# Gated cross-attention with a dense expert layer: the output projection as three fp32r products, and new places for the units beside the attention

## The chip, the core and the metric

The kernel runs on one core of a Trainium2 chip. The metric is the device time of one execution in microseconds (us). The engines of the core run their own instruction streams and meet at semaphores: TensorE (PE; its weight loads are listed apart, as PEld), VectorE (DVE), ScalarE (ACT), GpSimd (POOL) and SyncE (SP), which here issues all DMAs.

## The reference, cut to what matters

Batch 8, 512 queries and 512 keys for each, 256 channels, 16 heads of 16 channels, 8 experts with 1024 hidden channels. All is fp32.

```
def xattn(query, kv):
    q, k, v = query @ Wq + bq, kv @ Wk + bk, kv @ Wv + bv     # 16 heads of 16
    attn = softmax(clip(q @ k.T / 4, -1e4, 1e4))
    return (attn @ v) @ Wo + bo                               # output projection
x = x + tanh(g_xattn) * xattn(layernorm(x), ctx)
n = layernorm(x)
logits = n @ gate_weight.T                                    # kept if not under the 6144th smallest of 32768
y_e = gelu(n @ w1_e.T + b1_e) @ w2_e.T + b2_e                 # all 8 experts, dense
x = x + tanh(g_ffn) * sum_e(y_e * gate_e)
```

## The kernel before, in words

There are three stages. The first (lines 68 to 482) makes q, k and v of all batches and stores them in memory; each product is taken there in **fp32r**, a form of fp32 that TensorE takes in one pass with fewer bits, as three products of high and low parts (high by high, high by low, low by high), since operands are split by ScalarE (a copy into fp32r, the high part) and VectorE (the difference, the low part). The third stage is the experts, from about 560 us on.

The change is in the second stage, the attention (`attend_programs`, from line 643). For each of 8 batches it runs 4 groups `g` of 4 heads, each in 4 steps `k`, each with 4 places: 64 places in a batch, named `(g, k, place)`. At each place

- PE writes one turned score tile of the batch at hand into `ps_t` (line 862) and one score tile of 8 steps ahead into `ps_s` (line 851);
- ACT takes the exponential of the `ps_t` tile (line 1170, into `probs_T` or `w_raw`);
- DVE takes the least value of each row of the `ps_s` tile (`low`, line 1007).

`ps_t` and `ps_s` have 3 banks each, so PE can run three places ahead of ACT and DVE, no more. At place 3 of a step PE multiplies the probabilities of the step before by the values (`ps_o`, line 873, fp32).

All other work of a batch goes through one shared bank, `ps_m`, in units that are written into the stream at fixed places: the tables `SHARED` and `HALVES` say after which place PE writes a unit, `SCALAR_AT` and `VECTOR_AT` after which place ACT and DVE take it. Each entry is (kind, batch offset, index). The kinds: `low` (the least values, turned, line 879), `out` (heads turned, line 884, then normalised by DVE, lines 1025 to 1030), `rows` (the attention output turned, line 890, copied by ACT, line 1186), `y` (**the output projection**, line 898), after it DVE's residual add (line 1040), `statistics` (line 1048), `norm` (line 1082), the turned units `x2T` (905) and `xnT` (911), whose low part DVE makes (line 1091), `check` (lines 1013 and 1015), `logits` (919) and `pick` (926, once in four batches). Before a unit is written, PE waits for the unit before it in `ps_m` to be taken. The order on every engine is therefore written out by hand: an engine that waits at one unit holds up all that stands behind it.

The output projection before is one fp32 product: per batch 4 tiles of 128 queries by 2 halves of the channels, `attn_T` (fp32) by `wo` (fp32), 256 columns wide. TensorE carries each out as two recorded instructions. Two units `y` hold two tiles each; the first unit is cut into halves (`HALVES`), at two places. What belongs to the last batch has no further batch to lie beside: it is handed to the experts' programs as a list of closing pieces, and its units alternate between `ps_m` and `ps_o`.

`Wo` is loaded by SP in the first stage (line 175).

Of the kernel before, what the change touches and what calls it, by code (L numbers as in the profile page):

```python
# [549 lines left out]
VECTOR_AT = {  # L550
    (0, 1, 3): [("out", -1, 3)], (0, 2, 1): [("check", 0, 1)], (1, 0, 0): [("y", -1, 0)],
    (1, 0, 3): [("statistics", -1, 0), ("statistics", -1, 1)], (1, 1, 1): [("check", 0, 2), ("y", -1, 1)],
    (1, 1, 3): [("statistics", -1, 2), ("statistics", -1, 3)], (1, 2, 1): [("out", 0, 0)], (1, 3, 3): [("norm", -1, 0)],
    (2, 0, 1): [("norm", -1, 1)], (2, 0, 2): [("check", 0, 3)], (2, 1, 0): [("norm", -1, 2)], (2, 2, 1): [("out", 0, 1)],
    (2, 2, 2): [("norm", -1, 3)], (2, 3, 1): [("xnT", -1, 0)], (3, 1, 1): [("xnT", -1, 1)], (3, 2, 2): [("out", 0, 2)],
    (3, 3, 0): [("check", 1, 0)], (3, 3, 3): [("pick", -1, 0)],
# [3 lines left out]
    (0, 0, 3): [("copy", -1, 3), ("low", 0, 1)], (0, 2, 2): [("rows", -1, 0)], (0, 2, 3): [("rows", -1, 1)],  # L560
    (1, 1, 0): [("copy", 0, 0)], (1, 1, 2): [("low", 0, 2)], (1, 3, 2): [("x2T", -1, 0)],
    (2, 0, 3): [("x2T", -1, 1), ("copy", 0, 1)], (2, 1, 0): [("low", 0, 3)], (2, 3, 1): [("xnT", -1, 0)],
    (3, 0, 0): [("xnT", -1, 1)], (3, 0, 3): [("copy", 0, 2)], (3, 1, 2): [("low", 1, 0)], (3, 3, 0): [("logits", -1, 0)],
# [2341 lines left out]
```

## Time and profile before

| | us |
|---|---|
| median of 3 runs (lowest, highest) | 1897.73 (1895.09, 1897.74) |
| the profiled execution | 1896.23 |
| its span, first to last instruction | 1894.4 |
| PE busy, of the span | 1862.6 |
| DVE, ACT busy | 1291.1, 1277.7 |
| first stage | 0 to about 92 |
| attention | about 92 to 521 |
| experts | from there, alone from about 560 |

The page shows PE busy almost always. Matmuls are pipelined and their ends are modelled, so a full row of nines for PE does not say that PE has nothing to win or to lose: the spacing of its instructions and the idle time of the other engines have to be read beside it. TensorE's granted clock is at full speed except around 85 to 125 us.

### The profile page before, as it was taken

Reading aid. Unit: us, or ns where it says so; the run is one execution under the profiler, and the core shown is the slowest. Engines: PE = TensorE matmul, PEld = TensorE weight load, DVE = VectorE, ACT = ScalarE, POOL = GpSimd, SP = SyncE. Lnnn points to the kernel's source line nnn. Section 1 sums busy time; section 2 is a strip of 40 time slices with the busy share of each in tenths; the row PEclk is TensorE's granted clock in tenths of the full one; section 3 lists DMA queues with packets and bytes.
Section 4 is the critical chain, followed back from the end, with each engine's and each line's share of the span. In section 5 each row is a group of like instructions: output and inputs, shape, how many; then the busy total and the mean of one; then the engine's idle time right before and its main releaser. Section 6 shows DMA issues by size and latency. Waiting matters only on the chain.

```text
span 1894.4 us, 25738 instructions
## 1 busy us (share of the span) xinstructions
PE 1862.6 (98%) x8868; PEld 1349.0 (71%) x8868; DVE 1291.1 (68%) x2279; ACT 1277.7 (67%) x2145; POOL 146.9 (8%) x327
## 2 busy tenths in 40 slices
PE   7999999999999999999999999999999999999998
PEld 6844444444478777887888788788878888887886
DVE  6789999999666665656556666755665676556555
ACT  4447778777855556767666676766667676666665
POOL 6201101111135200000000000000000000000000
PEclk9969999999999999999999999999999999999999
DMA  8933333233113254333232333233233423222321
GB/s 284 374 81 84 87 91 88 79 88 110 38 50 129 107 210 151 119 117 110 90 111 89 133 138 124 95 112 112 89 112 129 151 93 117 111 90 89 121 101 58
DMA packets 97245, 220.84 MB, mean 117 GB/s; under 512 B 31314, under 2 KB 49492, under 8 KB 87892
## 3 DMA queue, kind: packets, MB, share of 16 engines
q1 hardware_dynamic: 97108, 219.12, 33.5%
q8 instruction: 73, 1.20, 0.3%
q14 instruction: 64, 0.52, 0.1%
HBM read 178.57 MB, written 40.24 MB: 116 GB/s over the span
## 4 chain that ended last, share of the span: by engine, by line
PE 89%; ACT 3%; DVE 2%; issue 1%; POOL 0%; ACTq 0%; DVEq 0%; POOLq 0%
PE ps_y L2169 32%; PE ps_h L2116 28%; PE ps_t L862 7%; PE ps_o L873 6%; PE ps_h L2089 5%; PE ps_y L2101 4%; PE ps_s L851 2%; PE ps_m L898 2%; PE ps_m L884 1%; ACT w_raw L1170 1%; DVE low L1007 1%; PE ps_m L890 0%; ACT gelu L2366 0%; PE ps_m L919 0%; PE ps_m L905 0%
## 5 line engine op out<-in xcount | busy, mean ns | idle before, releaser
L2469 DVE TENSOR_TENSOR h_lo<-gelu,h_hi 128x512 fp32r<-128x512 f32 x512 | 352.8, 693 | 437.0 <-ACT h_hi L2369 405.7
L2116 PE MATMUL ps_h<-x_hi,w_pair 128*128 128x512 f32 x1568 | 562.3, 392 | 1.8 <-ACT gelu L2366 0.8
L2366 ACT ACTIVATE gelu<-early,b 128x512 f32<-128x512 f32 x336 | 243.2, 724 | 229.5 <-DVE early L2618 220.7
L2116 PEld LDWEIGHTS ps_h<-x_hi,w_pair 128*128 128x128 f32 x1568 | 294.3, 188 | 78.3 <-issue 6.0
L1007 DVE TENSOR_REDUCE low<-ps_s 128x1 f32<-128x512 f32 x512 | 322.1, 681 | 26.1 <-PE ps_s L851 23.1
L2369 ACT ACTIVATE h_hi<-gelu 128x512 fp32r<-128x512 f32 x448 | 283.5, 633 | 41.9 <-ACT gelu L2366 1.1
L2116 PE MATMUL ps_h<-x_lo,w_pair 128*128 128x512 f32 x784 | 309.4, 395 | 0.0
L2618 DVE TENSOR_TENSOR early<-ps_h,copy 128x512 f32<-128x512 f32 x336 | 230.5, 686 | 49.4 <-PE ps_h L2116 49.4
L1170 ACT ACTIVATE probs_T<-ps_t 128x512 f32<-128x512 f32 x384 | 206.4, 594 | 45.5 <-PE ps_t L862 44.6
L851 PE MATMUL ps_s<-k_st,q_st 48*128 48x512 f32 x512 | 205.0, 481 | 3.2 <-SPq L755 2.0
L2169 PE MATMUL ps_y<-h_hi,w_lo 128*128 128x512 f32 x512 | 202.7, 396 | 0.0
L2169 PE MATMUL ps_y<-h_hi,w_hi 128*128 128x512 f32 x512 | 202.4, 395 | 0.0
L2169 PE MATMUL ps_y<-h_lo,w_hi 128*128 128x512 f32 x512 | 202.0, 394 | 0.0
L862 PE MATMUL ps_t<-q_st,k_st 49*128 49x512 f32 x512 | 190.4, 456 | 3.6 <-ACT probs_T L1170 2.7
L862 PEld LDWEIGHTS ps_t<-q_st,k_st 49*128 49x128 f32 x512 | 84.0, 188 | 131.8 <-ACT probs_T L1170 54.3
L2116 PEld LDWEIGHTS ps_h<-x_lo,w_pair 128*128 128x128 f32 x784 | 147.2, 188 | 32.7
L2169 PE MATMUL ps_y<-h_hi,w_first_lo 128*128 128x512 f32 x384 | 152.0, 396 | 0.0
L2169 PE MATMUL ps_y<-h_hi,w_first_hi 128*128 128x512 f32 x384 | 151.8, 395 | 0.0
L2169 PE MATMUL ps_y<-h_lo,w_first_hi 128*128 128x512 f32 x384 | 151.6, 395 | 0.0
L2169 PEld LDWEIGHTS ps_y<-h_hi,w_lo 128*128 128x128 f32 x512 | 96.2, 188 | 23.2
L2169 PEld LDWEIGHTS ps_y<-h_hi,w_hi 128*128 128x128 f32 x512 | 96.0, 188 | 22.8
L2169 PEld LDWEIGHTS ps_y<-h_lo,w_hi 128*128 128x128 f32 x512 | 96.1, 188 | 22.3
(263 smaller groups left out, 2536.4 us busy)
## 6 DMA issues: line engine op xcount, KB each, us to landing
x_hi<-blocks_scratch SPq DMA_DIRECT2D x28, 1024.0 KB, 5.2
x_lo<-blocks_scratch SPq DMA_DIRECT2D x28, 1024.0 KB, 8.8
x_hi<-blocks_scratch SPq DMA_DIRECT2D x28, 768.0 KB, 6.7
x_lo<-blocks_scratch SPq DMA_DIRECT2D x28, 768.0 KB, 10.2
gate<-gates_scratch SPq DMA_DIRECT2D x64, 256.0 KB, 3.2
q_st<-q_scratch SPq DMA_DIRECT2D x192, 64.0 KB, 2.3
k_st<-k_scratch SPq DMA_DIRECT2D x192, 64.0 KB, 2.3
k_scratch<-k_hl SPq DMA_DIRECT2D x8, 1024.0 KB, 5.6
```

The costliest lines, as they stand in the source:

```text
L851: pe.matmul(ps_s[bank_of(turn, at)][:], q_st[g][rows, j // 2, t * P:(t + 1) * P], k_st[g][rows, j // 2, :], start=True, stop=True).then_in ...
L862: pe.matmul(ps_t[bank_of(turn, at)][:], k_st[g][rows, j // 2, k * P:(k + 1) * P], q_st[g][rows, j // 2, :], start=True, stop=True).then_in ...
L873: mm = pe.matmul(ps_o[32 * j:32 * j + VW, :], v_st[g][:, k, j, :], probs_T[k][:, j, :], start=(k == 0), stop=(k == TT - 1))
L1007: dve.tensor_reduce(low[:, g % 2, column:column + 1], ps_s[bank_of(turn, at)][:], AX_X, ALU.min).then_inc(low_done, 1)
L1170: act.activation(probs_T[k][:, turned_head(b, g, k, i), :], ps_t[bank_of(turn, (g * TT + k) * GROUP + i)][:], ACT.Exp, scale=-1.0).then_in ...
L2089: mm = pe.matmul(ps_h[:, j % RING, :], w[:, k, at], x[:, k, bass.ds(c * SEQ, SEQ)], start=(i == 0), stop=(i == len(parts) - 1))
L2116: mm = pe.matmul(bank, w[wp], x[xp], start=start and n == 0, stop=n == 2, skip_group_check=not start)
L2169: mm = pe.matmul(ps_y[s][:, d, :], w[:, j, at], h[:, c, :], start=(i == 0 and c < 2 and m == 0), stop=(i == QUADS - 1 and c >= 2 and m == 2))
L2366: act.activation(gelu[:, c % GELUS, :], src, ACT.Gelu_apprx_tanh, bias=b1[p][:, j:j + 1]).then_inc(gelu_done, 1)
L2369: act.activation(h_hi[:, c, :], gelu[:, c % GELUS, :], ACT.Copy).then_inc(h_hi_done, 1)
L2469: dve.tensor_tensor(h_lo[:, j % RING, :], gelu[:, j % GELUS, :], h_hi[:, j % RING, :].bitcast(F32), ALU.subtract).then_inc(h_ready, 1)
L2618: dve.tensor_tensor(corner[c // 2], bank, copies[0 if c == 3 else 1][:], ALU.add).then_inc(corner_done, 1)
```

## The change

Four edits.

1. The output projection becomes three fp32r products, as elsewhere in the kernel. `Wo` is split once into `wo_hi` (ACT) and `wo_lo` (POOL). Each `rows` unit is copied by ACT into `attn_hi`, and DVE subtracts it from the bank into `attn_lo` (a new task `rows` for DVE, two in each batch); only then is the bank free and may PE begin `y`. `attn_lo` lies where `xn_b` lies.
2. `Wo` is loaded at the start of the attention instead of in the first stage, into the room of `attn`; PE and DVE wait for its split before the first batch.
3. The tables of places are new, for all units on PE, ACT and DVE.
4. `logits_T` keeps the logits of one group of four batches instead of two; ACT waits for `pick` before it overwrites them.

```diff
@@ project
-            sp.dma_start(keep["wo"][:], io["Wo"].rearrange("(k p) n -> p k n", p=P)).then_inc(wo_loaded, 16)
@@ tables
-HALVES = {(0, 3, 2): ("y", -1, 0)}
+HALVES = {(1, 0, 0): ("y", -1, 0)}
-    (1, 0, 0): ("y", -1, 0), (1, 1, 1): ("y", -1, 1), (1, 1, 3): ("low", 0, 2), (1, 2, 0): ("out", 0, 0),
+    (1, 0, 1): ("y", -1, 0), (1, 1, 1): ("y", -1, 1), (1, 1, 3): ("low", 0, 2), (1, 2, 1): ("out", 0, 0),
...
@@ sync
+        sp.dma_start(wo_raw, io["Wo"].rearrange("(k p) n -> p k n", p=P)).then_inc(wo_loaded, 16)
@@ gpsimd
+        pool.wait_ge(wo_hi_done, 1)
+        pool.tensor_tensor(wo_lo[:], wo_raw, wo_hi[:].bitcast(F32), ALU.subtract).then_inc(wo_split, 1)
@@ tensor
         def project_out(ps_m, b, i, tiles=range(2)):
             pe.wait_ge(taken["rows"], b * KT + KT)
+            parts = [(a, w, k) for k in range(KT) for a, w in ((attn_hi, wo_hi), (attn_hi, wo_lo), (attn_lo, wo_hi))]
             for t in tiles:
                 t0 = (2 * i + t) * P
-                for k in range(KT):
-                    mm = pe.matmul(ps_m[:, t * DIM:(t + 1) * DIM], attn_T[:, k, t0:t0 + P], wo[:, k, :],
-                                   start=(k == 0), stop=(k == KT - 1))
+                for n, (a, w, k) in enumerate(parts):
+                    mm = pe.matmul(ps_m[:, t * DIM:(t + 1) * DIM], a[:, k, t0:t0 + P], w[:, k, :],
+                                   start=(n == 0), stop=(n == len(parts) - 1))
...
+        pe.wait_ge(wo_split, 1)
@@ vector
+        def rows_low(b, i):
+            if i == 0:
+                wait(dve, in_psum["xnT"], b * KT)
+            dve.wait_ge(rows_hi_done, b * KT + i + 1)
+            dve.tensor_tensor(attn_lo[:, i, :], bank("rows", b, i)[:], attn_hi[:, i, :].bitcast(F32), ALU.subtract).then_inc(taken["rows"], 1)
...
         def set_flag():
+            for i in range(KT):
+                rows_low(LAST, i)
             dve.wait_ge(fits_in_psum, 1)
...
+        dve.wait_ge(wo_split, 1)
@@ scalar
         def take_rows(b, i):
-            act.activation(attn_T[:, i, :], bank("rows", b, i)[:], ACT.Copy).then_inc(taken["rows"], 1)
+            act.activation(attn_hi[:, i, :], bank("rows", b, i)[:], ACT.Copy).then_inc(rows_hi_done, 1)
         def take_logits(b, i):
+            if b % HELD == 0:
+                wait(act, in_psum["pick"], b // HELD)
...
+        act.wait_ge(wo_loaded, 16)
+        act.activation(wo_hi[:], wo_raw, ACT.Copy).then_inc(wo_hi_done, 1)
         take_lows(0, 0)
```

The first place is PE in batch 1, from the second half of the `rows` units to the first unit of `y`. Line 862 is the turned scores, 851 the scores ahead, 873 the product with the values, 890 a `rows` unit and 898 the projection. Before:

```order
L873 MATMUL ps_o<-probs_T,v_st 17x512 x4
L890 MATMUL ps_m<-ident,attn 128x128 x4
L862 MATMUL ps_t<-q_st,k_st 128x512
L851 MATMUL ps_s<-k_st,q_st 128x512
L862 MATMUL ps_t<-q_st,k_st 128x512
L851 MATMUL ps_s<-k_st,q_st 128x512
L862 MATMUL ps_t<-q_st,k_st 128x512
L851 MATMUL ps_s<-k_st,q_st 128x512
L898 MATMUL ps_m<-wo,attn_T 128x256 x2
L862 MATMUL ps_t<-q_st,k_st 128x512
L851 MATMUL ps_s<-k_st,q_st 128x512
```

Now, from the product with the values at the end of group 0 to the scores of place (1, 0, 1) (870, 859, 881 and 907 are the lines 862, 851, 873 and 898 of before):

```order
L881 MATMUL ps_o<-probs_T,v_st 17x512 x4
L870 MATMUL ps_t<-q_st,k_st 128x512
L859 MATMUL ps_s<-k_st,q_st 128x512
L907 MATMUL ps_m<-wo_hi,attn_hi 128x256
L907 MATMUL ps_m<-wo_lo,attn_hi 128x256
L907 MATMUL ps_m<-wo_hi,attn_lo 128x256
L907 MATMUL ps_m<-wo_hi,attn_hi 128x256
L907 MATMUL ps_m<-wo_lo,attn_hi 128x256
L907 MATMUL ps_m<-wo_hi,attn_lo 128x256
L870 MATMUL ps_t<-q_st,k_st 128x512
L859 MATMUL ps_s<-k_st,q_st 128x512
```

Half a `y` unit is two products of before and six now. The first half moved from the end of group 0 to behind the first place of group 1, and the second half of `rows` no longer follows the product with the values directly: one pair of scores stands between.

The second place is DVE at the same point. Line 1007 is the least values, 1013 and 1015 the check, 1040 the residual add and 1048 a statistics instruction. Before, from the normalisation of the last heads to the first residual add:

```order
L1030 TENSOR_TENSOR attn<-ps_m,recip 128x4x64
L1007 TENSOR_REDUCE low<-ps_s 128x1 x2
L1013 SCALAR_TENSOR_TENSOR fits<-low,fits 128x16
L1015 SCALAR_TENSOR_TENSOR fits<-low,fits 128x16
L1007 TENSOR_REDUCE low<-ps_s 128x1 x7
L1040 SCALAR_TENSOR_TENSOR x_res<-ps_m,tanh_g,x_res 128x512
```

Now (1017, 1023, 1025 and 1056 are the lines 1007, 1013, 1015 and 1040 of before; 1049 is new):

```order
L1017 TENSOR_REDUCE low<-ps_s 128x1 x3
L1049 TENSOR_TENSOR attn_lo<-ps_m,attn_hi 128x512
L1017 TENSOR_REDUCE low<-ps_s 128x1
L1023 SCALAR_TENSOR_TENSOR fits<-low,fits 128x16
L1025 SCALAR_TENSOR_TENSOR fits<-low,fits 128x16
L1017 TENSOR_REDUCE low<-ps_s 128x1 x2
L1049 TENSOR_TENSOR attn_lo<-ps_m,attn_hi 128x512
L1017 TENSOR_REDUCE low<-ps_s 128x1 x3
L1023 SCALAR_TENSOR_TENSOR fits<-low,fits 128x16
L1025 SCALAR_TENSOR_TENSOR fits<-low,fits 128x16
L1017 TENSOR_REDUCE low<-ps_s 128x1
L1056 SCALAR_TENSOR_TENSOR x_res<-ps_m,tanh_g,x_res 128x512
```

Two subtractions and a check now stand before the residual add, where only least values and one check stood.

## Rows read from the trace of the kernel before

**Rows 1.** Busy time by stage; the header names the columns.

```profile
core 0: us, PE busy (x) PEld busy (x) DVE busy (x) ACT busy (x) POOL busy (x), PEclk, DMA share, GB/s
0.00:60.00 60.00, 47.78 (x262) 40.20 (x263) 41.33 (x74) 28.49 (x35) 34.47 (x117) 1.00 0.89 295
...
250.00:300.00 50.00, 49.76 (x320) 22.24 (x312) 46.87 (x96) 38.99 (x79) 6.03 (x16) 1.00 0.32 87
...
700.00:1700.00 1000.00, 998.29 (x4291) 803.55 (x4290) 612.72 (x915) 692.00 (x1107) 0.00 (x0) 1.00 0.32 114
```

**Rows 2.** The same by three whole batches of the attention.

```profile
154.00:204.57 50.57, 50.32 (x322) 22.22 (x326) 47.41 (x97) 39.41 (x80) 6.04 (x16) 1.00 0.32 87
204.57:255.24 50.67, 50.43 (x324) 22.39 (x328) 47.53 (x98) 39.53 (x80) 6.05 (x16) 1.00 0.30 82
255.24:305.91 50.67, 50.42 (x324) 22.38 (x328) 47.54 (x98) 39.68 (x80) 6.03 (x16) 1.00 0.33 89
```

**Rows 3.** DVE by line, 154 to 306 us: count, busy, mean ns, idle.

```profile
L1007 DVE TENSOR_REDUCE low<-ps_s 128x1 f32<-128x512 f32 x193 | 122.0, 681 | 8.4 <-PE ps_s L851 7.1
...
L1040 DVE SCALAR_TENSOR_TENSOR x_res<-ps_m,tanh_g,x_res 128x512 f32<-128x512 f32 x6 | 4.5, 745 | 1.0 <-PE ps_m L898 1.0
...
L1091 DVE TENSOR_TENSOR x_lo<-ps_m,x_hi 128x512 fp32r<-128x512 f32 x6 | 4.1, 680 | 0.0
```

**Rows 4.** Waits 204.57 to 255.24 us: total us, times, longest.

```profile
PEld ps_t L862 <- ACT probs_T L1170: 6.5, 13, 0.9
...
PEld ps_s L851 <- DVE low L1007: 0.5, 2, 0.3
```

**Rows 5.** The chain, 200 to 260 us: start, us, what.

```profile
222.24 1.06 PE ps_m L898 x4
...
225.15 1.06 PE ps_m L898 x4
...
228.82 1.92 PE ps_m L898 x8
```

**Rows 6.** The chain, 480 to 560 us: the projection of the last batch.

```profile
524.07 1.73 PE ps_o L898 x8
525.80 1.74 PE ps_m L898 x8
```

**Rows 7.** PE in order of time, first stage: second and last of 24 products.

```profile
32.36 0.28 PE L275 MATMUL ps_v<-wv_lo,ctx_hi 128*128 128x256 f32 x1
...
34.94 0.28 PE L275 MATMUL ps_v<-wv_hi,ctx_lo 128*128 128x256 f32 x1
```

**Rows 8.** DVE in order of time, one batch: its idle time in brackets.

```profile
210.72 4.46 DVE L1007 TENSOR_REDUCE low<-ps_s 128x1 f32<-128x512 f32 x7 [0.52 <-PE ps_s L851]
215.42 2.48 DVE L1007 TENSOR_REDUCE low<-ps_s 128x1 f32<-128x512 f32 x4 [0.24 <-PE ps_s L851]
...
221.84 2.65 DVE L1007 TENSOR_REDUCE low<-ps_s 128x1 f32<-128x512 f32 x4 [0.76 <-PE ps_s L851]
225.30 0.69 DVE L1007 TENSOR_REDUCE low<-ps_s 128x1 f32<-128x512 f32 x1 [0.81 <-PE ps_s L851]
226.33 0.75 DVE L1040 SCALAR_TENSOR_TENSOR x_res<-ps_m,tanh_g,x_res 128x512 f32<-128x512 f32 x1 [0.33 <-PE ps_m L898]
```

**Rows 9.** Start of the attention, each engine in order of time.

```profile
94.09 0.62 SPq L758 DMA_DIRECT2D bo_gated<-in_bo  x1
...
103.14 0.27 ACT L1181 ACTIVATE low_rows<-ps_m 16x128 fp32r<-16x128 f32 x1 [11.74 <-PE ps_m L879]
...
112.37 0.62 PE L862 MATMUL ps_t<-q_st,k_st 49*128 49x512 f32 x1
```

**Rows 10.** The load of Wo on the page of DMA issues: KB, us to landing.

```profile
wo<-in_Wo SPq DMA_DIRECT2D x1, 256.0 KB, 4.5
```

**Rows 11.** POOL's bias add, twice as wide as the new subtraction: ns.

```profile
L831 POOL TENSOR_TENSOR x_res<-x_res,bo_gated x8: 2372/2386/2719, 161.1 to 505.0; 128x1024 f32<-128x1024 f32 x8
```

**Rows 12.** DVE and ACT in order of time, at the last batch's projection.

```profile
522.90 0.15 DVE L1109 TENSOR_SCALAR clip_flag<-ps_t 128x1 int32<-128x1 f32 x1
524.48 0.69 DVE L2469 TENSOR_TENSOR h_lo<-gelu,h_hi 128x512 fp32r<-128x512 f32 x1 [1.42 <-ACT h_hi L2322]
...
522.55 0.59 ACT L1186 ACTIVATE attn_T<-ps_m 128x512 f32<-128x512 f32 x1
```

More of the change, by code:

```diff
@@ L545 @@
+    (1, 0, 1): ("y", -1, 0), (1, 1, 1): ("y", -1, 1), (1, 1, 3): ("low", 0, 2), (1, 2, 1): ("out", 0, 0),
+    (1, 2, 3): ("x2T", -1, 0), (2, 0, 1): ("x2T", -1, 1), (2, 1, 1): ("low", 0, 3), (2, 2, 0): ("out", 0, 1),
+    (2, 3, 1): ("xnT", -1, 0), (3, 0, 1): ("xnT", -1, 1), (3, 1, 2): ("low", 1, 0), (3, 2, 1): ("out", 0, 2),
     (3, 3, 0): ("logits", -1, 0), (3, 3, 3): ("pick", -1, 0),
 }
-HALVES = {(0, 3, 2): ("y", -1, 0)}
+HALVES = {(1, 0, 0): ("y", -1, 0)}
 VECTOR_AT = {
[L551 to L556, printed above, removed]
+    (0, 1, 3): [("out", -1, 3)], (0, 2, 2): [("rows", -1, 0)], (0, 2, 3): [("check", 0, 1)], (0, 3, 1): [("rows", -1, 1)],
+    (1, 0, 0): [("check", 0, 2)], (1, 0, 1): [("y", -1, 0)], (1, 0, 3): [("statistics", -1, 0)],
+    (1, 1, 0): [("statistics", -1, 1)], (1, 1, 1): [("y", -1, 1)], (1, 1, 3): [("statistics", -1, 2)],
+    (1, 2, 0): [("statistics", -1, 3)], (1, 2, 1): [("out", 0, 0)], (1, 3, 3): [("check", 0, 3)],
+    (2, 0, 0): [("norm", -1, 0), ("norm", -1, 1), ("norm", -1, 2)], (2, 1, 3): [("norm", -1, 3)], (2, 2, 0): [("out", 0, 1)],
+    (2, 3, 2): [("xnT", -1, 0)], (3, 0, 2): [("xnT", -1, 1)], (3, 2, 1): [("out", 0, 2)], (3, 3, 2): [("check", 1, 0)],
+    (3, 3, 3): [("pick", -1, 0)],
@@ L557 @@
 }
 SCALAR_AT = {
[L560 to L563, printed above, removed]
+    (0, 0, 0): [("low", 0, 1)], (0, 0, 3): [("copy", -1, 3)], (0, 2, 0): [("rows", -1, 0)], (0, 3, 0): [("rows", -1, 1)],
@@ L564 @@
+    (1, 0, 3): [("copy", 0, 0)], (1, 1, 3): [("low", 0, 2)], (1, 2, 3): [("x2T", -1, 0)], (2, 0, 3): [("x2T", -1, 1)],
+    (2, 1, 0): [("copy", 0, 1)], (2, 1, 2): [("low", 0, 3)], (2, 3, 0): [("xnT", -1, 0)], (3, 0, 1): [("xnT", -1, 1)],
+    (3, 0, 3): [("copy", 0, 2)], (3, 1, 0): [("low", 1, 0)], (3, 3, 2): [("logits", -1, 0)],
 }
@@ L656, in attend_programs @@
     attn = n_.sb("attn", [P, TT, DIM])
-    attn_T = n_.sb("attn_T", [P, KT, SEQ])
+    wo_raw = attn[:, 0:KT, :]
+    attn_hi = n_.sb("attn_hi", [P, KT, SEQ], F32R)
+    with ExitStack() as lo_ctx:
+        attn_lo = Names(n_.nc, lo_ctx).sb("attn_lo", [P, KT, SEQ], F32R)
+    xn = n_.sb("xn_b", [P, TT, DIM])
     x_res = n_.sb("x_res", [P, TT, DIM])
     fits = n_.sb("fits", [P, 3, GROUP * TT])
-    xn = n_.sb("xn_b", [P, TT, DIM])
     stats = n_.sb("stats_b", [P, TT, 6])
@@ L925, in pick_logits @@
             for t in range(TT):
-                mm = pe.matmul(ps_m[:, t * COLUMNS:(t + 1) * COLUMNS], logits_T[:, b // HELD, t * P:(t + 1) * P],
+                mm = pe.matmul(ps_m[:, t * COLUMNS:(t + 1) * COLUMNS], logits_T[:, t * P:(t + 1) * P],
                                picks[:].rearrange("p i e -> p (i e)"), start=True, stop=True)
@@ L1107, in set_flag @@
         def set_flag():
+            for i in range(KT):
+                rows_low(LAST, i)
             dve.wait_ge(fits_in_psum, 1)
             dve.tensor_scalar(keep["clip_flag"][:], ps_t[BANKS - 1][:, 0:1], 3 * HEADS * TOKENS - 0.5, None, ALU.is_lt).then_inc(fits_summed, 1)
-        take = {"out": normalise, "y": add_residual, "xnT": split, "pick": keep_logits,
+        take = {"out": normalise, "rows": rows_low, "y": add_residual, "xnT": split, "pick": keep_logits,
                 "check": check_lows, "statistics": statistics, "norm": layer_norm}
@@ L1201, in take_logits @@
             act.wait_ge(in_psum["logits"], b + 1)
+            if b % HELD == 0:
+                wait(act, in_psum["pick"], b // HELD)
             rows = slice(b % HELD * COLUMNS, (b % HELD + 1) * COLUMNS)
-            act.activation(logits_T[rows, b // HELD, :], bank("logits", b, i)[rows, :], ACT.Copy).then_inc(taken["logits"], 1)
+            act.activation(logits_T[rows, :], bank("logits", b, i)[rows, :], ACT.Copy).then_inc(taken["logits"], 1)
         take = {"low": take_lows, "rows": take_rows, "x2T": take_x2, "xnT": take_hi, "logits": take_logits, "copy": copy_out}
@@ L2845, in build @@
         keep["k_st"] = [loads.sb(f"k_st{i}", [P, GROUP // 2, SEQ], F32R, "right") for i in range(GROUPS)]
-        keep["wo"] = loads.sb("wo", [P, KT, DIM], F32, "right")
+        keep["wo"] = [loads.sb(f"wo_{part}", [P, KT, DIM], F32R, "right") for part in ("hi", "lo")]
         keep["stored"] = [loads.sem(f"a_stored{i}") for i in range(2)]
```

14 lines of the change are left out of this document (7 added, 7 removed).

## The prediction

> **What bounds the kernel now.** I read the busy time by stage first. The change touches the attention alone, and the experts behind it keep PE busy 998.3 of 1000 us [rows 1]: what the attention gains or loses arrives at the end in full. Nothing behind it has slack to give or take.
>
> Within the attention I cut the trace at the same instruction of successive batches. A batch takes 50.67 us; PE shows 50.4 of it busy, DVE 47.5, ACT 39.5 [rows 2]. PE's figure contains the modelled tails of its instructions, so it can't tell what PE could still win. Three other views can. The chain of waits runs through the projection: its three pieces of a batch stand in it with 1.06, 1.06 and 1.92 us [rows 5]. DVE's idle time of a batch is (8.4 + 1.0) / 3 = 3.1 us, nearly all of it waiting for PE's scores [rows 3]. And that idle time isn't spread: of one batch 0.52 + 0.24 + 0.76 + 0.81 + 0.33 = 2.66 us lie between 210 and 226 us, around the `rows` units and the two halves of the first `y`, and none above 0.1 us from there to the batch's end at 255 [rows 8]. PE waited there for DVE's least values 0.5 us [rows 4]. So PE sets the pace in the first part of a batch, where it does `rows` and `y`, and in the other 29 us DVE is full and PE and DVE go nearly level. The second `y` unit (228.8 us) stands just inside that full stretch.
>
> **The products.** Before, 16 recorded instructions per batch. In the last batch, where they follow each other closely, 8 take 1.73 us, 0.217 each [rows 6]; in the loop 4 take 1.06 and 8 take 1.92, which is 4 or 8 times 0.217 plus 0.19 for the change of work [rows 5]. After, 24 products of 128x256 in fp32r per batch. The first stage has exactly this form, at full clock [rows 1, 7]: from the second to the last of 24 are 22 steps in 34.94 - 32.36 = 2.58 us, 0.117 each. Per batch 16 x 0.217 = 3.47 becomes 24 x 0.117 = 2.81, 0.66 less: 0.17 for each half and 0.33 for the full unit. Over 8 batches PE wins 5.3 us at most.
>
> A page of the Trainium skill, "FP8 and Floating Point Precision", section TensorE Precision Notes, counts true fp32 as four passes through the array. By that three products would cost 3/4 of one fp32 product, 0.87 us less per batch instead of 0.66. The rows say 2.81 / 3.47 = 0.81, since a product of 256 columns costs 0.117 us each time where a pass of the fp32 form costs 0.217 / 2 = 0.109; I take the rows.
>
> **DVE's subtraction.** It has the form of line 1091 (128x512, bank minus high part into fp32r), busy 4.1 / 6 = 0.68 us [rows 3]. Two per batch are 1.36 us, onto 47.5. DVE's floor becomes 48.9 plus the 3.1 - 2.66 = 0.5 us of small gaps that it shows even where it is full: 49.4 us. PE's side gives 50.67 - 0.66 = 50.0. DVE's floor is lower, so the subtraction is hidden if it lies where DVE idles. It does for the most part: the new entries stand at (0, 2, 2) and (0, 3, 1), in the stretch with the 2.66 us of idle. Without that cover it costs up to 1.36 us per batch. What is queued behind it: if ACT's high part comes late, DVE stands at the subtraction and the least values behind it stand too, and after three places PE stands for their banks. ACT copies a unit now directly at its place instead of two places later, and has 11 us free in a batch, so I put this wait at nothing.
>
> **What is kept of the gain.** Seven batches have their projection inside the loop. The halves lie in PE's stretch: 2 x 0.17 x 7 = 2.4 us, kept. The full unit lies where DVE is full; what PE wins there it can only use as far as DVE has least values' banks to free. I keep half: 0.33 x 7 / 2 = 1.2 us (bounds 0 and 2.3).
>
> **The new places.** The `rows` units and the halves have a pair of scores between them and the product with the values, so PE feeds DVE where it starved it: 0.76 us of DVE's idle time stand right behind the two `rows` units [rows 8]. The other tasks keep their kind and number; three `norm` now stand together on DVE at (2, 0, 0), and both halves of `y` fall into group 1, which was PE's longest. No row prices this. Its ends are the idle time that is there to recover, 2.66 - 1.36 = 1.3 us per batch, and on the other side the same 1.3 us lost if tasks collide. I take 0.07 gained per batch, 0.5 us in all, since most of the idle time that a smoother order could use is filled by the subtraction.
>
> **The start.** The load of Wo is issued behind `bo`, whose issue ends at 94.7 us; with 4.5 us to landing it is there at about 99.7 [rows 9, 10], though two value loads and twelve score loads come behind it. ACT's split is one copy of 128x512, 0.6 us as in [rows 12], done by 100.4. ACT's next work begins only at 103.1 [rows 9]: hidden with 2.7 us to spare. If the load came 5 us late, the low rows, and with them the first turned scores, would be late by 2 us. POOL's subtraction is half as wide as the bias add, so about 1.2 us [rows 11]: done by 102, 10 us before PE's first turned scores at 112.4. SP is held 0.6 us longer before the loads of group 2, which PE wants at 112. The load that leaves the first stage saves it one issue and 256 KB of loads [rows 10] where its DMA share is 0.89 [rows 1]; PE had enough to do by then. I put the start at 0 (bounds -0.5 and +2).
>
> **The end of the attention.** ACT's second copy ends at 523.14; DVE's subtractions start at 522.9 behind the h_lo instruction that ends there, and end 2 x 0.65 later at 524.2 or so [rows 12]. PE began its projection at 523.9: it waits about 0.4, and has 0.66 less to do [rows 6]. The flag instruction moves behind; DVE was idle for 1.42 us there, so the next h_lo isn't late. Net 0.2 less at most; I take 0.1. The wait for `pick` before `logits_T` is reused falls in batch 4 and was met many us earlier: nothing.
>
> **Sum.** -2.4 - 1.2 - 0.5 + 0 - 0.1 = -4.2 us. The durations are of the profiled execution: 1896.2 us, of which the span is 1894.4, so 1892.0 for it. The median of the runs is 1.5 us above it; the forecast for a median is 1897.7 - 4.2 = 1893.5.
>
> **Rivals.**
>
> *A, PE keeps all.* The full unit is kept whole (+1.1) and the new order recovers 0.3 us more idle time in each batch. For it: PE has its projection in the chain of waits three times per batch [rows 5], and PE waited only 0.5 us for DVE [rows 4]. Against: DVE would have to run at 48.9 of 49.7. Time: -4.2 - 1.1 - 2.1 = -7.4, 1890.3.
>
> *B, DVE takes it back.* The subtractions fall before a DVE that has a backlog, and the gain of PE turns into PE's waiting for banks of `ps_s`. Of the products only the halves' 2.4 us are kept, and 0.3 us in each batch is lost to subtractions that find no idle time. For it: the 29 us without idle time [rows 8]. Time: -2.4 + 2.1 = -0.3, 1897.4.
>
> *C, slower: DVE is the bound.* The page "Perfetto Trace Analysis" of the Trainium skill (section Identifying the Most-Contended Engine) says to judge DVE by its busy share and not to judge TensorE by its matmul's. By that rule DVE, 94% busy in a batch while PE's weight loads show 44% [rows 2], is the engine that counts, and a change that hands it more work is a loss. As a mechanism of this kernel: DVE meets each subtraction in order, and its wait for PE's `rows` unit and ACT's copy adds to it, so the 1.36 us come on top of the idle time instead of into it; the least values fall behind by more than the three banks hold, and PE stops. The place is (0, 2, 2) to (1, 0, 0) of each batch. It decides once less than half of the 1.36 us finds idle time: 1.36 per batch minus the 0.34 of the halves, over 7 batches, is +7.1, 1904.8. Against it: the idle time stands just there, and PE's wait for DVE is small.
>
> *D, the start waits for Wo.* +2 us as above on the forecast, 1895.5, and part of it is in the range. The clock of TensorE is no rival: it is at full speed in the whole steady stretch [rows 1, 2].
>
> **Chances.** The forecast (between -2.5 and -5.8) 0.36, A 0.22, B 0.22, C 0.14, D 0.06. A measurement of this kernel tells 0.2%, 3.8 us, from no change; the forecast lies close to that bound. Faster by more: A whole, 0.22, and somewhat over six tenths of the forecast's 0.36, 0.24: 0.46. Slower by more: C and a little of B: 0.16. Within: 0.38. The range reaches past A and half way into C: 1888 to 1901.
>
> **What would show it.** In the new trace: 24 instructions of the projection in a batch, 0.117 apart; the pieces in the chain 0.89, 0.89 and 1.6 us long; DVE busy 48.9 in a batch of 50.0 to 50.3; its idle time between the `rows` and the first `y` down from 2.66 to about 1; PE's wait for DVE's least values up from 0.5 us, but under 1.5. The first turned scores at 112.4. B shows as that wait above 2 us with the batch still at 50.6; C as a batch above 51 and idle time of DVE that ends at ACT's copy into `attn_hi`. I am wrong in the mechanism if the batches don't change while the total does, or if the projection's instructions aren't 0.117 apart.

## The result: 0.5% slower, by a collision that the prediction did not have

| | before | changed |
|---|---|---|
| median of 9 runs, us | 1897.72 (1895.09 to 1899.18) | 1904.56 (1903.62 to 1912.46) |
| span of the profiled execution, us | 1894.4 | 1902.7 |
| PE, DVE, ACT, POOL busy, us | 1862.6, 1291.1, 1277.7, 146.9 | 1862.2, 1306.6, 1282.6, 147.7 |

The ratio is 1.0051, interval 1.0043 to 1.0059. I had forecast 1893.5, with a range of 1888 to 1901, and gave 0.16 to a time above it. The busy times of the whole tell nothing of it: PE is 0.4 us less busy, DVE 15.5 us more.

The experts are as full as they were in [rows 1]; three batches of the attention, cut as in [rows 2] at the first turned scores of each, are not alike any more. Columns: stretch, its length, busy time of PE, PEld, DVE, ACT, POOL with instructions, granted clock, DMA share, GB/s.

```profile
160.40:212.38 51.98, 50.28 (x332) 22.11 (x328) 50.07 (x99) 39.43 (x78) 6.67 (x17) 1.00 0.31 83
212.38:263.75 51.37, 50.30 (x333) 22.09 (x329) 49.45 (x99) 40.01 (x80) 5.08 (x17) 1.00 0.31 84
263.75:317.46 53.71, 51.67 (x332) 22.68 (x328) 50.64 (x99) 40.42 (x80) 6.69 (x17) 0.97 0.30 81
700.00:1700.00 1000.00, 998.25 (x4290) 804.23 (x4289) 614.97 (x917) 691.07 (x1104) 0.00 (x0) 1.00 0.31 114
```

Batches of one program that does the same work in each took 50.7 before; now they take 51.98, 51.37 and 53.71, and DVE's busy time varies with them for the same 99 instructions. So some instruction of DVE does not take the same time in each batch. The rows of one line, grouped (duration in ns: least, median, most), name it. Changed, then before:

```profile
L1023 DVE SCALAR_TENSOR_TENSOR fits<-low,fits x32: 164/171/1861, 102.4 to 500.2; 128x16 f32<-128x16 f32 x32
```

```profile
L1013 DVE SCALAR_TENSOR_TENSOR fits<-low,fits x32: 159/163/175, 102.7 to 494.0; 128x16 f32<-128x16 f32 x32
```

It is the first instruction of `check`, 16 columns, with operands and result in SBUF. Seven of the 32 took 1.75, 0.90, 1.86, 1.19, 0.58, 1.13 and 0.86 us, one at each seam between two batches, 7.15 us above the usual 0.16 in sum. The longest one, on DVE in order of time (start, us, what):

```profile
262.43 1.29 DVE L1017 TENSOR_REDUCE low<-ps_s 128x1 f32<-128x512 f32 x2 [0.74 <-PE ps_s L859]
263.63 1.86 DVE L1023 SCALAR_TENSOR_TENSOR fits<-low,fits 128x16 f32<-128x16 f32 x1
265.42 0.16 DVE L1025 SCALAR_TENSOR_TENSOR fits<-low,fits 128x16 f32<-128x16 f32 x1
```

And POOL, then PE, at the same time:

```profile
263.09 2.37 POOL L839 TENSOR_TENSOR x_res<-x_res,bo_gated 128x1024 f32<-128x1024 f32 x1 [23.65 <-DMA x_res<-in_x]
```

```profile
264.09 0.39 PE L859 MATMUL ps_s<-k_st,q_st 48*128 48x512 f32 x1
...
266.33 0.27 PE L887 MATMUL ps_m<-ident,low 128*16 128x128 f32 x1 [1.85 <-DVE low L1017]
```

POOL's bias add of the next batch runs from 263.09 to 265.46; the check starts inside it and ends at 265.49, with it. All seven long checks do so: each ends 0.02 to 0.04 us after the bias add beside it. DVE can't clear the banks of the scores meanwhile, and PE stood for 1.85 us. The granted clock fell behind the wait: 1.00 in the 4 us with the wait, then 0.93, 0.50 and 0.72, though PE was busy again.

```profile
262.00:266.00 4.00, 2.48 (x18) 0.78 (x18) 3.57 (x5) 2.76 (x5) 2.37 (x1) 1.00 0.33 117
266.00:268.00 2.00, 1.67 (x13) 0.70 (x13) 2.00 (x5) 1.36 (x4) 0.00 (x0) 0.93 0.51 132
268.00:270.00 2.00, 2.00 (x10) 0.83 (x6) 1.01 (x2) 1.34 (x3) 0.00 (x0) 0.50 0.32 99
270.00:272.00 2.00, 2.00 (x12) 1.03 (x14) 1.63 (x4) 1.38 (x4) 0.00 (x0) 0.72 0.33 74
```

In the kernel before the two did not touch. At the seam shown here the check was over by 210.2 and the bias add began at 211.47; over the seven seams the distance was 1.0 to 3.9 us. DVE, then POOL:

```profile
209.95 0.16 DVE L1013 SCALAR_TENSOR_TENSOR fits<-low,fits 128x16 f32<-128x16 f32 x1
```

```profile
211.47 2.39 POOL L831 TENSOR_TENSOR x_res<-x_res,bo_gated 128x1024 f32<-128x1024 f32 x1 [24.16 <-DMA x_res<-in_x]
```

The change moved the check of group 0 from place (3, 3, 0) to (3, 3, 2). The excerpt of the diff ahead of the prediction leaves that line out; x1 below shows it. I gave it no price.

### The profile page after: what moved, and what is told of

Its sections match the earlier page's. It is cut to its first block, busy times and chain, and to the rows that moved or that the text cites. A ratio compares the mean times of both kernels' runs of the same rounds, so it can differ in the third digit from the quotient of the medians.

```text
span 1902.7 us, 25893 instructions
## 1 busy us (share of the span) xinstructions
PE 1862.2 (98%) x8932; PEld 1349.3 (71%) x8932; DVE 1306.6 (69%) x2295; ACT 1282.6 (67%) x2146; POOL 147.7 (8%) x328
## 4 chain that ended last, share of the span: by engine, by line
PE 71%; ACT 2%; DVE 1%; issue 1%; POOL 0%; ACTq 0%; DVEq 0%
PE ps_y L2192 32%; PE ps_h L2139 28%; PE ps_h L2112 4%; PE ps_y L2124 4%; PE ps_t L870 1%; PE ps_o L881 1%; ACT gelu L2389 0%; DVE early L2641 0%; ACT probs_T L1189 0%; DVE out_T_acc L2583 0%; ACT w_pair L2337 0%; PE ps_m L907 0%; PE ps_m L892 0%; DVE gated L2576 0%; ACT h_hi L2392 0%
```

## The experiments

Each is compared with runs of the kernel before on the same chip (median 1896.4 to 1896.7). Times of a group are from the first turned scores of a group to those of the next, in batch 2.

**x1: the check back at its old place, all else as changed.**

```
VECTOR_AT of the changed kernel
-    ..., (3, 2, 1): [("out", 0, 2)], (3, 3, 2): [("check", 1, 0)],
+    ..., (3, 2, 1): [("out", 0, 2)], (3, 3, 0): [("check", 1, 0)],
```

> The changed kernel with one entry moved back: DVE's check of the next batch's group 0 at (3, 3, 0) instead of (3, 3, 2). Theory P (the check has two operands in SBUF and is held while POOL's bias add of 2.4 us runs, 0.4 to 1.7 us in each of 7 batches, and PE and its clock suffer behind it): the long checks are gone, group 0 of a batch falls from 12.4-14.8 us to about 11.4, and the time falls by 7 to 11 us, to about 1895. Rival Q (DVE is simply too full with two more subtractions per batch, the held check only uses time that DVE would lose anyway): the time stays within 2 us of the changed kernel's 1904.6.

Median 1898.24 over 10 runs, ratio 1.0005 (0.9995 to 1.0015): the loss is gone, and no gain stands in its place. From 1.0051 to 1.0005 it is 8.7 us, inside the 7 to 11 of theory P. The new tables leave little room even so: the bias add begins at most 1.1 us behind this check, and once 0.05 us before its end, where the second instruction, already running, kept its 0.17 us. The check is 0.16 everywhere, batches are 50.68 and 50.63.

```profile
L1023 DVE SCALAR_TENSOR_TENSOR fits<-low,fits x32: 161/166/176, 102.6 to 495.8; 128x16 f32<-128x16 f32 x32
```

```profile
163.39:214.07 50.68, 50.50 (x332) 22.13 (x329) 48.71 (x99) 39.30 (x78) 6.82 (x17) 1.00 0.31 85
214.07:264.70 50.63, 50.44 (x332) 22.15 (x328) 48.78 (x99) 39.87 (x80) 5.29 (x17) 1.00 0.31 86
```

**x2: the kernel before with only the check moved late.**

```
VECTOR_AT of the kernel before
-    (3, 3, 0): [("check", 1, 0)], (3, 3, 3): [("pick", -1, 0)],
+    (3, 3, 2): [("check", 1, 0)], (3, 3, 3): [("pick", -1, 0)],
```

> The kernel before with one entry changed, the same check moved from (3, 3, 0) to (3, 3, 2); no product, no subtraction. Theory P: the check now meets POOL's bias add here too, and the kernel becomes slower by 0.5 to 1.5 us in each of 7 batches, 4 to 9 us in all. Rival Q: nothing changes, within 1 us, since DVE has as much work as before.

Median 1914.76 over 4 runs (1911.75 to 1921.74), ratio 1.0084 (1.0067 to 1.0101): one entry of a table costs 16 us by the ratio, 18 by the medians, and theory P had said 4 to 9. DVE, POOL and PE at the first collision:

```profile
165.10 0.16 DVE L1013 SCALAR_TENSOR_TENSOR fits<-low,fits 128x16 f32<-128x16 f32 x1
165.18 2.36 DVE L1015 SCALAR_TENSOR_TENSOR fits<-low,fits 128x16 f32<-128x16 f32 x1
```

```profile
165.12 2.39 POOL L831 TENSOR_TENSOR x_res<-x_res,bo_gated 128x1024 f32<-128x1024 f32 x1 [63.83 <-DMA x_res<-in_x]
```

```profile
168.20 0.52 PE L851 MATMUL ps_s<-k_st,q_st 48*128 48x512 f32 x1 [1.80 <-DVE low L1007]
```

Here POOL began between the two instructions of the check, and the second was held over the whole of it. PE waited 1.8 us there; most of the price of this seam came with the clock behind it:

```profile
165.00:168.00 3.00, 1.40 (x13) 0.48 (x5) 3.00 (x4) 1.78 (x4) 2.39 (x1) 1.00 0.40 130
168.00:171.00 3.00, 2.80 (x12) 0.71 (x12) 2.54 (x5) 0.60 (x1) 0.00 (x0) 0.59 0.46 135
171.00:176.00 5.00, 5.00 (x24) 1.98 (x20) 2.86 (x7) 2.92 (x6) 0.00 (x0) 0.50 0.14 30
176.00:181.00 5.00, 5.00 (x28) 2.20 (x24) 3.08 (x7) 2.66 (x5) 0.00 (x0) 0.72 0.01 2
181.00:186.00 5.00, 5.00 (x30) 2.40 (x28) 3.27 (x5) 3.26 (x6) 0.00 (x0) 1.00 0.06 16
```

PE does 24 instructions in 5 us at 0.50 and 30 at 1.00. Group 0 of batch 1 took 19.01 us instead of 12.63, the other groups of that batch what they took before. The clock fell behind four more of the six collisions of this execution; in the changed kernel it fell behind one of seven.

**x3: the changed kernel with the bias added on 16 of 256 columns** (the other 240 are left out), so POOL holds for 0.32 us.

```
-            pool.tensor_tensor(x_res[:], x_res[:], bo_gated...
+            pool.tensor_tensor(x_res[:, :, 0:16], x_res[:, :, 0:16], bo_gated[:, 0:16]...
```

> The changed kernel with all its places, but POOL adds the gated bias to 16 of 256 columns only (the rest of the bias is left out), so its instruction shrinks from 2.4 us to some 0.3. Theory P: the long checks are gone with the table untouched, and the time is that of the run with the check moved, about 1895. Rival Q: 1904 as the changed kernel. A third possibility, that the place itself costs something beside the collision, would show as a time between the two.

Median 1897.07 over 10 runs, 1.0003 (0.9993 to 1.0012). The check stands at its late place and takes at most 0.177 us. So it is the overlap with POOL that makes it long, not its place as such. Batch by batch, the changed kernel minus x3 is 1.3, 0.8, 3.0, 1.0, 0.0, 0.9 and 0.6 us, for holds of 1.6, 0.7, 1.7, 1.0, 0.4, 1.0 and 0.7: most of a hold arrives in the time, and the one with the fall of the clock behind it cost 1.3 us more than its length.

```profile
L1023 DVE SCALAR_TENSOR_TENSOR fits<-low,fits x32: 161/166/177, 102.6 to 492.8; 128x16 f32<-128x16 f32 x32
```

**x4: the three products with the old places**, the subtractions at (0, 2, 2) and (0, 3, 0).

```
changed kernel, tables of the kernel before, and:
+VECTOR_AT: (0, 2, 2): [("rows", -1, 0)], (0, 3, 0): [("rows", -1, 1)]
```

> The changed kernel with the tables of the kernel before, and the two subtractions put on DVE at (0, 2, 2) and (0, 3, 0): product and subtraction alone, without the new places. Theory P: no check meets the bias add; PE wins up to 0.66 us per batch and loses what waiting for the subtractions costs, so the time is 1893 to 1898, at most that of before. Rival Q: the subtractions cost DVE up to 1.36 us per batch also here: 1900 to 1906.

Median 1907.74 over 4 runs, 1.0056 (1.0039 to 1.0072): no check is held, and yet it is the slowest form of the product, above the 1906 at which the slower theory ended. Batches are 51.85 and 51.91. PE stands in two places that x1 doesn't have:

```profile
221.68 0.69 DVE L1048 TENSOR_TENSOR attn_lo<-ps_m,attn_hi 128x512 fp32r<-128x512 f32 x1
222.43 0.66 PE L897 MATMUL ps_m<-ident,attn 128*128 128x128 f32 x4 [0.55 <-DVE attn_lo L1048]
...
224.19 0.68 DVE L1048 TENSOR_TENSOR attn_lo<-ps_m,attn_hi 128x512 fp32r<-128x512 f32 x1
...
225.02 0.36 PE L906 MATMUL ps_m<-wo_hi,attn_hi 128*128 128x256 f32 x1 [1.03 <-DVE attn_lo L1048]
```

The bank of `rows`, and the projection's operand, now come back over ACT and DVE instead of ACT alone. With the old spacing PE waits for that path. The product needs a wider spacing of `rows` and `y`, whatever else the tables do: x11 has the old tables with that spacing, and its group 0 takes 12.63 us instead of 14.13.

**x5: the new places with the fp32 product of before**, the check early.

```
kernel before, tables of the changed kernel, and:
-    (3, 3, 2): [("check", 1, 0)]        VECTOR_AT also without ("rows", -1, 0), ("rows", -1, 1)
+    (3, 3, 0): [("check", 1, 0)]
```

> The kernel before with the new places on all engines (the check at (3, 3, 0), away from the bias add), but the fp32 product and no subtraction. The run with the product in the old places lost 1.25 us per batch, so if the subtraction's hand-over is what costs and the new places are what pays it back, this kernel is faster than before: 0.5 to 1.2 us per batch, 1889 to 1893. If instead the new places bring nothing by themselves and only fit the new product, it stays within 2 us of before's 1896.6.

Median 1899.09 over 10 runs, 1.0011 (1.0001 to 1.0020). The places alone lose, 51.11 a batch against 50.65, and 2.4 us by the medians, just above the 2 us of the second branch.

```profile
212.29:263.40 51.11, 50.92 (x325) 21.72 (x321) 47.83 (x97) 39.87 (x80) 5.29 (x17) 1.00 0.30 85
```

**x6: x1 without the two subtractions** (the low part of the attention's output is left out; the third product is high times high and has the same form, and ACT's copy frees the bank as before the change).

```
-            parts = [... ((attn_hi, wo_hi), (attn_hi, wo_lo), (attn_lo, wo_hi))]
+            parts = [... ((attn_hi, wo_hi), (attn_hi, wo_lo), (attn_hi, wo_hi))]
-            for i in range(KT):
-                rows_low(LAST, i)
```

> The changed kernel with the check moved to (3, 3, 0) and DVE's subtraction of the rows left out: the third product uses the high part again, ACT's copy frees the bank (the low part of the attention output is left out). Price of the subtraction: against the run with the check moved (steady batch 50.65 us), theory S (DVE full: each subtraction costs what it takes) gives 1.2 to 1.4 us less per batch, 49.3, and 1.4 us less at the end of the attention, 1886 to 1888; theory H (hidden, as I had forecast) gives less than 0.3 us per batch.

Median 1895.47 over 10 runs, 0.9993 (0.9984 to 1.0003). A batch takes 50.47. Inside a batch, x5 and x6 differ in the products alone (`Wo`'s load and the smaller `logits_T` also come with the changed kernel), and x6 and x1 in the subtractions.

```profile
161.50:211.97 50.47, 50.28 (x334) 21.96 (x330) 47.80 (x97) 39.32 (x78) 6.61 (x17) 1.00 0.32 85
```

**x7: the changed kernel, its check with one operand in SBUF** (the check isn't accumulated over the heads, and the flag is constant).

```
-            dve.scalar_tensor_tensor(out=fits[:, 0, :], in0=low[...], scalar=FITS, in1=fits[:, 0, :], ...)
+            dve.tensor_scalar(fits[:, 0, :], low[:, g % 2, :], FITS, None, ALU.is_le)
```

> The changed kernel as it is, places included, but DVE's two check instructions take one tensor operand instead of two (they no longer add up over the groups; the flag that they feed is fixed at not set). If only an instruction with two operands in SBUF is held by POOL's bias add, the long checks are gone and the time is about 1897. If any DVE instruction that reads and writes SBUF is held, the check stays 0.4 to 1.9 us long in every batch and the time stays at 1904.

Median 1905.97 over 4 runs, 1.0051 (1.0031 to 1.0071). It is held as long as the form with two operands. DVE, then POOL:

```profile
160.08 1.95 DVE L1023 TENSOR_SCALAR fits<-low 128x16 f32<-128x16 f32 x1
```

```profile
159.62 2.38 POOL L839 TENSOR_TENSOR x_res<-x_res,bo_gated 128x1024 f32<-128x1024 f32 x1 [57.76 <-DMA x_res<-in_x]
```

The idea that dropping one operand frees DVE is refuted for this form. The least values, which read a bank of PSUM, keep their 0.68 us each beside the same bias add in all these traces; no run tells whether that is because they reduce or because they read PSUM.

**x8: x1 with the first half of `y` one place earlier.**

```
-HALVES = {(1, 0, 0): ("y", -1, 0)}
+HALVES = {(0, 3, 3): ("y", -1, 0)}
```

> The changed kernel with the check moved to (3, 3, 0) and the first half of the first y unit one place earlier, at (0, 3, 3), so that group 1 of a batch no longer holds both halves. Group 1 took 14.65 us in the run with the check moved, group 0 11.72. If group 1 is long because PE's units crowd there while DVE starves, the sum of both falls by 0.3 to 0.8 us per batch, to 1892 to 1896; if the sum is set by DVE's work, 26.4 us stay 26.4; if PE then waits for the second subtraction, it rises.

Median 1896.28 over 10 runs, 0.9995 (0.9985 to 1.0004). Group 1 fell from 14.65 to 13.55 and group 0 rose from 11.71 to 12.59; the batch went from 50.63 to 50.43. A half unit costs where it stands, and its place is worth 0.2 us, below the 0.3 to 0.8 that I had hoped for.

**x9: x1 with the three `norm` of (2, 0, 0) apart.**

```
-    (2, 0, 0): [("norm", -1, 0), ("norm", -1, 1), ("norm", -1, 2)],
+    (2, 0, 0): [("norm", -1, 0)], (2, 0, 2): [("norm", -1, 1)], (2, 1, 0): [("norm", -1, 2)],
```

> The changed kernel with the check moved to (3, 3, 0) and the three norm instructions that stand together at (2, 0, 0) spread to (2, 0, 0), (2, 0, 2) and (2, 1, 0). Group 2 took 11.76 us with the old places and 11.98 with the new ones, with or without the product. If the three together are what costs (1.4 us of DVE in one piece, more than a bank of least values has room for), group 2 returns to about 11.8 and a batch to 50.45; the time falls by 1.5 us. If it is another move (the check that left group 2, x2T), nothing changes.

Median 1896.62 over 10 runs, 1.0004 (0.9994 to 1.0014). Group 2 stayed at 11.96 us (11.98 in x1, 11.76 before): the norms standing together are not what costs the 0.2 us there. What does, one of the other moves of that group, stays open. In this profiled execution, and in that of x10, the granted clock fell for some 3 us behind `pick`, at about 365 us, with no check held and no wait of PE above 1 us; batch 5 took 52.05 and 51.89 us there, against 50.63 in x1. Why it falls in some executions stays open. The stretch in x10:

```profile
366.00:370.00 4.00, 4.00 (x24) 1.69 (x20) 2.62 (x6) 2.55 (x6) 0.00 (x0) 0.63 0.50 133
```

**x10: x1, x8 and x9 together, and an early start of the last projection:** in the last batch PE begins it on the high parts, and waits for the low ones only before the last products of the first tile. The products stand in this new order in every batch.

```
+                pe.wait_ge(rows_hi_done, b * KT + KT)        (last batch, i == 0)
-            parts = [... for k in range(KT) for a, w in (...)]
+            parts = [... for a, w in (...) for k in range(KT)]
+                    if first and t == tiles[0] and n == 2 * KT:
+                        pe.wait_ge(taken["rows"], b * KT + KT)
```

> All that helped together: the changed kernel with the check at (3, 3, 0), the first half of y at (0, 3, 3), the norms apart, and in the last batch PE begins the projection with the products that need only the high part. Steady batch 50.2 to 50.45 against before's 50.69, 2 to 3 us in seven batches, 0.7 in the first; the end of the attention gives back 0.5 to 1 of the 1.4 us that the subtractions cost there, so it stays 0.4 to 0.9 us behind before. Together 2 to 4 us faster than before: 1893 to 1895. If the parts don't add up, it is 1896, as the run with the half moved.

Median 1895.5 over 11 runs, 0.9991 (0.9982 to 1.0000), just outside the 1893 to 1895 expected. From the last turned scores to PE's first work behind the last projection it is 13.03 us, against 13.64 in x1.

**x11: the tables of the kernel before, with only the edited units moved**, and the early start of x10.

```
changed kernel, tables of the kernel before, and:
+SHARED:    (0, 3, 0): ("rows", -1, 1), (1, 0, 1): ("y", -1, 0)
+HALVES:    (0, 3, 3): ("y", -1, 0)
+SCALAR_AT: (0, 2, 0): [("rows", -1, 0)], (0, 3, 0): [("rows", -1, 1)]
+VECTOR_AT: (0, 2, 2): [("rows", -1, 0)], (0, 3, 1): [("rows", -1, 1)], (1, 0, 1): [("y", -1, 0)]
```

> The changed kernel with the tables of before, except that rows and the halves of y stand as in the best run (rows at (0, 2, 2) and (0, 3, 0), the first half at (0, 3, 3), the second at (1, 0, 1)), and with the same early start of the last projection. If all the rest of the new places is worth nothing or less, as the run with the new places and the fp32 product says (51.10 us a batch against 50.69), this is as fast as the best run or faster: a batch of 50.1 to 50.4, 1892 to 1895. If the rest was chosen to fit the hand-over of the subtraction, it is slower: PE waits for the second subtraction as in the run with the product in the old places, up to 51 us a batch, 1899.

Median 1892.76 over 11 runs, 0.9984 (0.9975 to 0.9993): faster than both kernels, than the one before by 0.16%. Batches are 50.16 and 50.15, and from the last turned scores to the work behind the projection it is 12.57 against 13.02 before.

```profile
161.44:211.60 50.16, 49.93 (x332) 22.45 (x328) 48.52 (x99) 39.30 (x79) 6.36 (x17) 1.00 0.33 86
211.60:261.75 50.15, 49.90 (x332) 22.43 (x329) 48.58 (x99) 39.52 (x80) 6.33 (x17) 1.00 0.32 86
```

The groups of batch 2 side by side, in us; the last column is from the start of the last turned scores of the attention to PE's first instruction behind the last projection:

| | group 0 | 1 | 2 | 3 | batch | end of the attention |
|---|---|---|---|---|---|---|
| before | 12.61 | 14.04 | 11.76 | 12.23 | 50.65 | 13.02 |
| changed | 12.44 | 14.65 | 11.96 | 12.32 | 51.37 | 13.64 |
| x3, no collision | 11.70 | 14.63 | 11.98 | 12.28 | 50.60 | 13.65 |
| x4, old places | 14.13 | 13.65 | 11.86 | 12.26 | 51.91 | 13.08 |
| x5, places alone | 11.53 | 15.27 | 11.98 | 12.32 | 51.11 | 13.58 |
| x6, no subtraction | 11.53 | 14.63 | 11.99 | 12.31 | 50.45 | 13.13 |
| x11 | 12.63 | 13.50 | 11.78 | 12.25 | 50.15 | 12.57 |

## Why the prediction was wrong

The spans differ by 1902.7 - 1894.4 = 8.3 us. The traces divide it. The loop is taken here from the first turned scores of batch 1 to the last ones of batch 7: 352.81 before, 355.96 in x5, 351.56 in x6, 352.78 in x3, 360.28 changed.

| part | from | us | forecast |
|---|---|---|---|
| first turned scores | 112.10 against 112.37 | -0.3 | 0 |
| first batch | 48.30 against 48.96 | -0.7 | 0 |
| new places | x5 against before | +3.2 | -0.5 |
| products in the loop | x6 against x5 | -4.4 | -3.6 |
| subtractions in the loop | x3 against x6 | +1.2 | 0 |
| check held by the bias add | changed against x3 | +7.5 | not seen |
| end of the attention | 13.64 against 13.02 | +0.6 | -0.1 |
| experts | 1358.68 against 1358.38 | +0.3 | 0 |
| behind PE's last instruction | 9.69 against 8.89 | +0.8 | 0 |
| sum | | +8.2 | -4.2 |

The row of the first batch can't be put down to the change. TensorE runs at half clock there until 124.8 us before and 124.4 changed, and the batch's length goes with the moment at which the clock rises: 51.17 us in x1, where it rises at 133.0, and 46.54 in x9, at 119.6.

*The products were right.* I gave them 0.66 us a batch; x6 against x5 is 50.45 against 51.11, and nearly all of it lies in group 1, 15.27 to 14.63. In x1 the three pieces of the chain of waits that were 1.06, 1.06 and 1.92 us in [rows 5] are

```profile
226.28 0.91 PE ps_m L907 x6
227.62 0.90 PE ps_m L907 x6
...
230.83 1.61 PE ps_m L907 x12
```

against the forecast of 0.89, 0.89 and 1.6. Without the subtractions the full unit is kept whole too, 4.4 us over the loop. My 3.6 was meant with a DVE that has the subtractions to do, and what is left then is 3.2 (x3 against x5). The 1.2 us that I took off the full unit are what the subtractions cost: the sum of both terms is nearly right, with the loss on the wrong one.

*The subtractions were nearly hidden.* I said DVE has the idle time for them, and for most of it it has: 1.36 us more work cost 0.17 us a batch (1.2 over seven). DVE's idle time from the `rows` to the first `y` went from 2.66 in [rows 8] to 0.60 + 0.23 + 0.17 + 0.27 = 1.27 in x1, and it was 48.7 busy, as forecast 48.9. PE's wait for the least values rose from 0.5 to 1.1 us there, below the 1.5 that I had named:

```profile
PEld ps_s L859 <- DVE low L1017: 1.1, 3, 0.5
```

*The new places were mis-sized*, the step "I take 0.07 gained per batch". They lose 0.45. I read from the order that PE would feed DVE better behind the `rows` units. Group 0 is faster by 0.9 to 1.1 us, but that is no sign of it: with the half of `y` back in group 0 and the new spacing of `rows` kept, x8 has 12.59 there against 12.61 before (products and subtractions included; the spacing wasn't run by itself). Both halves of `y` fell into group 1, which I had named as PE's longest and then gave no price. It rose by 1.2, group 2 by 0.2 and group 3 by 0.1. The net of groups 0 and 1 is 0.15 us, so the larger part of the loss lies in groups 2 and 3, and which move makes it isn't shown; x9 cleared only the three `norm`.

*What was missed is the check.* "The other tasks keep their kind and number" was the step that failed, since it put the moved check at nothing where the runs show 7.5 us: a task of the same kind and number has another neighbour when it is moved, and the neighbour may be on an engine that no table orders. The trace before had it all: POOL's line 831 in [rows 11], 2.39 us on SBUF, and the check ending 1.0 to 1.3 us ahead of it at six of seven seams. It even had one instruction of DVE that was held, in the last batch: line 1863 subtracts 128x1024 with both operands in SBUF and took 3.30 us beside the bias add, where its other execution took 1.23. DVE, then POOL:

```profile
505.47 3.30 DVE L1863 TENSOR_TENSOR w_first_lo<-early,w_first_hi 128x1024 fp32r<-128x1024 f32 x1
```

```profile
504.96 2.72 POOL L831 TENSOR_TENSOR x_res<-x_res,bo_gated 128x1024 f32<-128x1024 f32 x1 [12.55 <-DMA x_res<-in_x]
```

None of my rivals was this one. I had named 1.3 us a batch as the worst end of the places, 9.1 over seven batches, and then let the range end at 1901, which doesn't hold it. Places and collision together took 3.2 + 7.5 = 10.7 us, beyond even that end. The Trainium skill, "SBUF — State Buffer", section Who interferes with whom, states it: GpSimd shares a pair of ports with DVE, and an instruction of DVE with two inputs in SBUF that is issued second is blocked fully, not slowed, while GpSimd reads SBUF. The traces agree: 1.86 and 2.36 us for an instruction of 0.16, ending with POOL's, and 0.17 for the one in x1 that had begun first. The same section lets `tensor_scalar` contend through a two-port mode, and a reduction never; x7's 1.95 us and the least values' steady 0.68 agree with both, though no trace shows the mode, and the least values read PSUM.

*The end of the attention was wrong in sign.* The chain of the changed kernel runs through it:

```profile
529.99 1.29 DVE attn_lo L1049 x2
531.42 1.67 PE ps_o L907 x12
```

ACT's second copy starts at 529.64, the first subtraction at 529.99 behind an `h_lo`, and PE 0.14 us after the second. This is the last batch, and little lies beside it: in the last column of the table above the subtractions cost 0.5 us (13.13 in x6 to 13.64 or 13.65 in x3 and the changed kernel), the products win 0.45 (13.58 in x5 to 13.13), and the new places, which I had not counted here at all, cost 0.56 (13.02 to 13.58). I forecast 0.4 us of waiting for the subtraction, which is about right; what I missed here was again the price of the places. That PE can begin on the high parts wins 0.6 us (x10), and with the old places the end is shorter than before (x11; with the old places and no early start it is 13.08, in x4).

*Two small rows stay open.* From the first expert's work to PE's last instruction it is 0.3 us more, over 1358 us; and from PE's last instruction to the end 9.69 instead of 8.89, while x2, x5 and x6 have 8.83 and the others 9.1 to 9.6. DVE's and PE's last instructions are the same there, and the 0.8 us lie behind DVE's last one. What makes them isn't shown; no run was made on it.

*The start was right.* Wo was there for ACT at 99.38 and POOL's low part took 1.27 us at 100.25 (forecast about 1.2):

```profile
99.38 0.63 ACT L1238 ACTIVATE wo_hi<-attn 128x512 fp32r<-128x512 f32 x1 [8.21 <-DMA attn<-in_Wo]
```

```profile
100.25 1.27 POOL L803 TENSOR_TENSOR wo_lo<-attn,wo_hi 128x512 fp32r<-128x512 f32 x1
```

*Rival C gave the time, 1904.8, by luck and not by its cause.* Its sign was to be batches above 51 with idle time of DVE that ends at ACT's copy into `attn_hi`. The batches are above 51, yet without the collision DVE does the same instructions in 50.6, so the higher busy time of DVE is no bound. Only x4 comes near to C, and there too PE waits for `attn_lo` (two waits of 0.55 and 1.03 us) and not for the least values, 0.5 us as before. The medians differ by 1904.56 - 1897.72 = 6.8 us, less than the 8.3 of the spans by the 1.5 us that the profiled execution of the kernel before lies below its median.

## What to carry to other kernels

When a table moves an instruction, look at its new neighbours on every engine, above all at what POOL does on SBUF then: a small instruction of DVE that is long once in 32 times is found by the least and the most duration of its line, not by a mean. A split into high and low parts costs little in DVE's busy time if a place is free, and much in the path from engine to engine: widen the distance between its steps (x11 against x4), and cut that path where the last one stands alone (x10, x11). When units change their cost, move those units and leave the rest: the old tables with six entries moved and two added gave 1892.76 (x11), the new tables with the check early and the same start of the last projection 1895.50 (x10), and the new tables as they were 1904.56.

## What the runs showed of the hardware

- An instruction of DVE of 0.16 us, operands and result in SBUF, that starts inside POOL's elementwise add takes until that add ends: up to 2.36 us with two operands, up to 1.95 with one. The add beside a held check stays at 2.37 to 2.42 us. In the last batch before, it took 2.72 beside a conversion and a subtraction of 128x1024, and the subtraction took 3.30 instead of 1.23.
- A wait of PE of 1.8 us was followed by a granted clock of 0.50 for some microseconds, in x2 from 171 to 176 with PE busy all the time. The 2.4 us of a hold became 6.4 us of group 0 there. The wait alone doesn't decide: in the changed kernel a wait of 1.85 us was followed by a fall and one of 1.50 us, ending at 162.6, was not.
- A product of 128x256 in fp32r costs 0.117 us, in place of two records of 0.217 us for 256 columns in fp32: three for one is 0.81 of the time, and not 0.75.
